# An attention and mixture-of-experts kernel: two key tiles of weights times values side by side in every second odd slot, and a rotary product one slot earlier

## What is computed

```python
x = x + attn(layernorm(x)); x = x + ffn(layernorm(x))
# attn, for each batch b:
ct_q, ct_kv = x @ Wd_q + b, x @ Wd_kv + b
query = ct_q @ Wu_q + rope(ct_q @ Wq_r)
key   = ct_kv @ Wu_k + rope(x @ Wk_r)
value = ct_kv @ Wu_v
out   = softmax(query @ key.T / scale) @ value @ Wo
```

## Time and profile before

| | |
|---|---|
| three timed runs | 584.26, 586.39, 596.13 us; median 586.39 |
| profiled execution | 590.88 us |
| its span, first to last instruction | 589.0 us |
| PE busy | 512.5 us, 87% |
| DVE busy | 391.2 us, 66% |
| ACT busy | 345.5 us, 59% |
| POOL busy | 350.2 us, 59% |
| L622, weights times values | 1024 instructions, 82.6 us |
| L1021, maxima on DVE | 256 instructions, 689 ns each |
| L855, exponentials on ACT | 256 instructions, 592 ns each |

### The profile page before, as it was taken

One profiled execution on the slowest core, in us unless ns is written; L12 is line 12 of the kernel. 1 busy time (PEld: TensorE's weight loads), 2 busy tenths in 40 slices (PEclk: granted clock), 3 DMA queues, 4 the chain that ended last, 5 costly groups with the idle time before them and its releaser, 6 DMA issues.

```text
span 589.0 us, 16333 instructions
## 1 busy us (share of the span) xinstructions
PE 512.5 (87%) x4222; PEld 368.7 (63%) x4223; DVE 391.2 (66%) x1173; ACT 345.5 (59%) x881; POOL 350.2 (59%) x617
## 2 busy tenths in 40 slices
PE   4579899999999999999999967999699999999800
PEld 2336555665556555655554424998599999999800
DVE  5567577887888788878885753667445555555446
ACT  1216577777777777677765645455355555555642
POOL 7564545676777677767774535477645555555521
PEclk9757899999999999999997986899989999999955
DMA  6224445455545554554556366322422222221084
GB/s 247 69 78 124 129 134 151 137 165 150 146 146 163 152 147 141 162 158 143 175 163 200 92 223 216 88 75 88 176 75 58 57 59 58 65 62 43 1 255 172
DMA packets 64753, 75.78 MB, mean 129 GB/s; under 512 B 11778, under 2 KB 51851, under 8 KB 64064
## 3 DMA queue, kind: packets, MB, share of 16 engines
q1 hardware_dynamic: 59552, 64.49, 36.6%
q0 software_dynamic: 5152, 10.70, 5.2%
HBM read 51.25 MB, written 25.08 MB: 130 GB/s over the span
## 4 chain that ended last, share of the span: by engine, by line
PE 61%; DMA 9%; DVE 9%; POOL 7%; issue 7%; SPq 4%; ACT 1%; DVEq 1%; POOLq 0%; ACTq 0%
PE s L820 12%; PE s L828 12%; PE pv L622 8%; PE s L591 8%; PE s L610 6%; DMA w<-mrow 2%; POOL dispatched L1561 2%; PE pb L646 2%; DVE w L1469 2%; DVE mx L1021 2%; PE pb L647 2%; PE pm L600 1%; DMA weighed_out<-weighed_sb 1%; SPq L426 1%; PE pb L655 1%
## 5 line engine op out<-in xcount | busy, mean ns | idle before, releaser
L1021 DVE TENSOR_REDUCE mx<-s 128x2 f32<-128x512 f32 x256 | 175.4, 689 | 63.1 <-PE s L591 61.1
L855 ACT ACTIVATE pr<-s 128x512 f32<-128x512 f32 x256 | 149.9, 592 | 88.5 <-PE s L610 86.9
L996 ACT ACTIVATE pr<-s,wts 128x128 f32<-128x128 f32 x352 | 100.4, 368 | 85.8 <-PE s L820 85.8
L1681 POOL DMA_INDIRECT results<-pr,ridx x88 | 96.4, 1096 | 76.9 <-DVE pr L1433 48.5
L610 PE MATMUL s<-w 75*128 75x256 bf16 x512 | 102.9, 284 | 6.4 <-DMA w<-mrow 6.1
L591 PE MATMUL s<-w 72*128 72x256 bf16 x512 | 104.6, 288 | 1.3 <-DVE mx L1021 1.2
L828 PE MATMUL s<-w,pr 128*128 x704 | 94.9, 279 | 1.3 <-ACT pr L996 1.3
L828 PEld LDWEIGHTS s<-w,pr 128*128 128x128 f32 x704 | 87.5, 196 | 1.7 <-issue 1.7
L622 PE MATMUL pv<-pr,vm 128*32 128x256 f32 x1024 | 82.6, 409 | 0.0
L1561 POOL DMA_INDIRECT dispatched<-pay,pos x64 | 64.1, 1002 | 30.1 <-issue 11.3
L591 PEld LDWEIGHTS s<-w 72*128 72x128 bf16 x512 | 40.4, 103 | 58.2 <-issue 34.0
(11 more groups left out here) (180 smaller groups left out, 763.4 us busy)
## 6 DMA issues: line engine op xcount, KB each, us to landing
w<-in_w SPq DMA_DIRECT2D x20, 512.0 KB, 4.3
w<-parts_out SPq DMA_DIRECT2D x32, 288.0 KB
w<-parts_out SPq DMA_DIRECT2D x96, 96.0 KB
parts_out<-qkp SPq DMA_DIRECT2D x16, 384.0 KB
tin<-dispatched SPq DMA_DIRECT2D x88, 66.0 KB, 1.8
weighed_out<-weighed_sb SPq DMA_DIRECT2D x16, 256.0 KB
w<-results SPq DMA_DIRECT2D x8, 512.0 KB, 7.8
outT<-weighed_out SPq DMA_DIRECT2D x16, 128.0 KB
```

The costliest lines, as they stand in the source:

```text
L855: nc.scalar.activation(pr[h // NG % 2][:, h % NG, :, :], s2[h % 2][:, :, :], ACT.Exp, scale=SCALE).then_inc(exp_done, 1)
L996: last = nc.scalar.activation(hT[t.pair][:, c, :], hps[t.pair][:, :, :].rearrange("p a s -> p (a s)")[:, c * P:(c + 1) * P], ACT.Gelu, bia ...
L1021: nc.vector.tensor_reduce(mx[j % 2][:, :, g], s1[h % 2][:, :, :], AX.X, ALU.max).then_inc(max_done, 1)
L1681: nc.gpsimd.indirect_dma_start(results, bass.IndirectOffsetOnAxis(ap=ridx[t.slot][:, 0:1], axis=0), yo[t.slot], None, bounds_check=TOPK * ...
```

## The change

In quarters 1 to 3 of a step, weights times values of the quarter before stood with its two key tiles in slots g = 1 and g = 3 (slots 5 and 7, 9 and 11, 13 and 15). Now both key tiles stand in slot g = 1 (5, 9, 13), as those of the last quarter already did in slot 1 of the next step. Rotary product 1 moves from slot 13 to slot 12. Nothing is computed otherwise, and only PE's program changes.

```diff
                     if h == 1 and held.weigh:
                         for t in range(QT):
                             weigh(b - 1, 1 - s, NQ - 1, t)
-                    if q > 0 and g % 2 == 1 and held.attend:
-                        weigh(b, s, q - 1, g // 2)
+                    if q > 0 and g == 1 and held.attend:
+                        for t in range(QT):
+                            weigh(b, s, q - 1, t)
...
                         elif h == 10:
                             compress(b + 3)
-                        elif h == 13:
+                        elif h == 12:
                             wait(pe, ct_done, b + 4)
                             rotary(b + 3, 0, r1_full, pb)
```

## The result

| | before | changed |
|---|---|---|
| time, median | 586.39 us (584.26 to 596.13) | 594.51 us (593.73 to 597.70) |
| profiled run | 590.88 us | 594.86 us |
| its span | 589.0 us | 593.0 us |
| granted clock, mean | 0.918 | 0.924 |
| period of a middle step | 19.54 us | 20.07 us |

The changed kernel takes 1.017 times as long, 95% interval 1.010 to 1.024: 8.1 us more by the medians, 4.0 by the two profiled runs. One further run of the kernel before took 1609 us and is in no figure here, and every ratio compares fast runs alone. That is a little slower, and less than the 2% that the prediction named as the least that can be told from no change; the interval leaves out 1. The row to compare with the earlier trace rows is that of the same stretch, slot 0 to slot 0.

The account below looks back on a forecast made before the run. The prediction took PE as the bound (busy 19.11 of 19.60 us). To the median of 586.39 us it added 8.3 for the steps and 8.5 for the clock, giving 603.2 us, with a range of 588 to 618.

Parts of the forecast that it names:

- rival B: Product in slot 12: ct is late but the clock stays, 586.4 + 8.3 = 594.7 us; chance 0.25.
- A: The forecast itself: ct is late and some steps fall to half clock, 603 us, range 597 to 612; chance 0.48.
- A pair costs 1.00 and saves 0.23: Slots 5, 9, 13: a pair of key tiles takes 1.00 us, and each saves PE 0.23 us of its own time.
- The pair in slot 5 is swallowed by L600's wait: Slot 6: the pair's 0.43 us goes into the wait of 0.49 for POOL, so slot 7 starts unchanged.
- Slot 8 waits for the copy of the values: Slot 8: transposes of x wait for ACT's copy, so of 0.66 us sooner only 0.08 is left.
- PE reaches the product far ahead of ct: Slot 12: PE comes to the rotary product at 235.62 instead of 237.26 and waits 1.31 us for ct.
- Ct comes 0.21 later than before: DVE's maximum of slot 6 starts 0.21 us later and this goes down the chain: ct done 236.87, before 236.66.
- The sum without the clock, +8.3: Whole run: steps 2 to 12 lose 8.4 us (0.76 each), steps 0 and 1 lose 1.2, steps 13 to 15 gain 1.3.
- The clock, +8.5: Waits at the product: 5 of 13 bring a short stretch at half clock, 1.7 us each, +8.5 us.
- The sign: Whole kernel: slower, chance 0.60; within 2%, 0.34; faster, 0.06.
- The rule of the skill that I kept as a rival: Wait at the product: only idle gaps clearly longer than this cost the clock, so the sum stays at +8.3 us.

Follow-up runs that it names:

- bias-first experiment: Changed kernel with POOL's addition of the output bias put ahead of its subtraction: 628.32 us, 1.038 of the kernel before.
- ct later: Changed kernel with an extra 512-column activation into a spare buffer on ACT ahead of ct: 623.58 us, 1.035 of the kernel before.
- ct sooner: Changed kernel with ACT making ct behind the exponential of slot 10 instead of 11: 615.14 us, 1.024 of the kernel before; on another chip 617.47 us, 1.016.

## Why the prediction was right, and where it was not

The number, 603, stands 8 us above the result and the result lies inside the range; but the case that came true is rival B (594.7: ct is late, the clock stays), not A. That B's figure is met to 0.2 us is luck: its terms are off by several us either way (points 5 and 6), and the two profiled runs, which alone can be read term by term, differ by 4.0 and not by 8.1. Point by point:

1. *A pair costs 1.00 and saves 0.23.* Right: 234.00 to 235.00, and the bare slot 7 lasts 0.44 (236.43 to 236.87).
2. *The pair in slot 5 is swallowed by L600's wait.* Right: no wait is left there, and slot 7 starts 8.99 us behind the step's start (236.43 - 227.44), against 9.01 before.
3. *Slot 8 waits for the copy of the values.* Right: L636 starts 10.63 behind the step's start, before 10.65; it marks the 0.60.
4. *PE reaches the product far ahead of ct.* Right: slot 12's passes end at 242.12, 14.68 into the step (forecast 14.62), and PE stands there, the transposes of x2 and slot 13 behind it.
5. *Ct comes 0.21 later than before.* **Wrong, the term that was mis-sized in the step.** Ct is done at 243.08, 15.64 into the step; before it was 15.66. DVE's maximum of slot 6 did start 0.21 later against the step (235.43, 7.99 in, before 7.78), but the sum of marks behind it took up the delay. I took DVE's work between two maxima as fixed. It was not: before, the sum held 0.60 us, and it ended with POOL's subtraction. Rows of the kernel before, DVE and then POOL:

```profile
229.77 0.60 DVE L1116 TENSOR_TENSOR chosen<-oh 128x48 bf16<-128x48 f32 x1
```

```profile
229.15 1.15 POOL L1520 TENSOR_TENSOR work<-work,qkp 128x512 f32<-128x512 f32 x1
```

and after:

```profile
236.43 0.36 DVE L1117 TENSOR_TENSOR chosen<-oh 128x48 bf16<-128x48 f32 x1
```

```profile
235.57 1.15 POOL L1521 TENSOR_TENSOR work<-work,qkp 128x512 f32<-128x512 f32 x1
```

Before: DVE's end 230.37, POOL's 230.30. After: 236.79 and 236.72. DVE ends 0.07 behind POOL both times, so its later start costs nothing. The Trainium skill, "SBUF — State Buffer", section "SBUF: two separate sides", says that a VectorE operation with two inputs in SBUF and a GpSimd one that reads SBUF lock each other out; both traces and the bias-first experiment (1.06 us) agree. The chain from there went with POOL, which hadn't moved. So the wait is 1.01 by starts and not 1.31, the step 20.07 and not 20.30: **+0.53 us, not +0.76**.
6. *The sum without the clock, +8.3.* Of the 11 middle steps 0.51 each by the starts of the slot-1 pairs (219.57 against 213.91 us, from 89.68 and 87.00 to 309.25 and 300.91): 5.7, forecast 8.4. From slot 1 of step 1 to that of step 2 it lost 2.8, where I had 1.2 for steps 0 and 1: slot 6's turning waits 2.15 instead of 1.71 in step 1, and the half-clock stretch there lasts 6.8 us instead of 3.4. The last pair is 6.7 later than the last tile was before (368.35, 361.65), so steps 13 to 15 gave back 1.6, forecast 1.3; but in that stretch the changed kernel spent 17.1 us at half clock and the kernel before 22.4, so what the pairs gave there isn't shown. The end is only 4.0 later. Behind the last pair the changed kernel spent 38.9 us at half clock against 43.0, worth up to 2.1 of these 2.7 us, with no cause in the change that I can show.
7. *The clock, +8.5.* **Wrong, the larger error.** In the profiled run not one of the thirteen waits was followed by the lower clock. Two things failed. The wait was 0.85 as marked, since point 5 shortened it, and stood nearer to the 0.99 of the earlier trace rows that did no harm than to the 1.37 that I compared it with; I also set a wait by starts (1.31) against one as marked (1.37), two measures that differ by 0.16 here. And a stretch costs about 1.1 us and not the 1.7 of half its length, by the steps of ct later. By that experiment (waits of 1.13 to 1.51) the forecast would have been 4 of 13 stretches at 1.1, +4.4, had the wait really been at 1.3. And that the clock stayed is partly luck: on two later chips the same kernel had three stretches at half clock in each trace between 160 and 320 us, five of the six in slot 0 some 5 us behind such a wait at the product, one at a wait of 1.11. The rule of the skill that I kept as a rival gave the right number here, though it fails on the others (below).
8. *The sign.* Right, and the halves show why: the pairs alone 1.002 and 1.005, the move alone 1.016.

On two of the three later chips the same change was run as it is, and costs 3.2 and 3.4%: the late results come on top (one more microsecond a step), and the three stretches at half clock. The trace of before that I had could show no late results, since none was in it.

## What to carry to other kernels

- A producer's slack is what a move spends. Ct had 0.60 us in hand, and PE came to the product 1.64 sooner; of the 0.69 us that the pairs take off PE only 0.24 shows even without the move. Read who is released last at the new place before counting what the edit saves.
- An instruction of DVE with two inputs in SBUF beside a long one of POOL has no duration of its own: take its end from POOL's end, and ask which of the two moves.
- Compare a wait with waits of the same measure (as marked, or by starts), and take the price of a fallen clock from a step's length, not from the length of the stretch.

## What the runs showed of the hardware

- **The port lock.** A sum of DVE over 48 columns took 0.36 to 1.06 us in the three places above, and ended 0.06 to 0.07 us behind POOL's instruction in each; in the changed kernel's middle steps it takes 0.29 to 0.37 with the same 0.06 to 0.07, and at 334.22 and 354.73, where POOL has no subtraction, 0.19.
- **The clock.** Over fourteen traces, marked waits of PE between 62 and 300 us and whether the granted clock fell to 0.50 (1.2 GHz) during or right behind them: under 0.75 us, 2 of 243; 0.75 to 1.0, 2 of 31; 1.0 to 1.2, 6 of 17; 1.2 to 1.5, 3 of 8; longer, 11 of 24. The four of the shortest two groups were all waits in slot 0, some 5 us behind one of about 0.86 at the product. So it is a chance and not a sharp limit: almost none under 1.0 us, about four in ten above, where these counts are too few to tell the three groups apart. The Trainium skill's abstract rule, in "TensorE: Matmul & The Clock Gate", section "HAM oscillation", by which only gaps longer than any of these cost the clock, does not hold here.
- **Late results.** In the twelve traces of three chips PE's results reached DVE up to 1.6 us late (and ACT too: in the step of ct sooner shown above an exponential starts at 241.15, 0.97 behind its pass 2 instead of 0.42), only while POOL issued indirect sends, and moving the sends moved the late slots. Shown is the tie in time; what holds the results, and why the two traces of the first comparison have none, stays open.
